# Moving the loads of two experts and of six bias rows behind another load in a mixture-of-experts kernel

## The reference

```python
def _L1_ffn_ref(x, Wr, We, be):          # x 16x256x512, Wr 512x8, We 8x512x512, be 8x512
    logits = jnp.einsum('bsd,de->bse', x, Wr)
    w, sel = jax.lax.top_k(logits, 2)
    w = jax.nn.softmax(w, axis=-1)
    gate = jnp.einsum('bsk,bske->bse', w, jax.nn.one_hot(sel, E, dtype=w.dtype))
    for e in range(E):
        out = out + gate[..., e:e + 1] * (jnp.einsum('bsd,df->bsf', x, We[e]) + be[e])
x = x + _L0_ffn_ref(_L0_cond_ref(x, ...), w1, w2, w3)
x = x + _L1_ffn_ref(_L1_cond_ref(x, cond), Wr, We, be)
```

## Time and profile before

| | us |
|---|---|
| median of three runs | 831.52 (828.22 to 833.4) |
| the profiled execution, device time | 832.25 |
| its span, first to last instruction | 830.5 |
| PE busy | 737.6 (89%) |
| DVE busy | 564.7 (68%) |
| POOL busy | 476.9 (57%) |
| ACT busy | 397.6 (48%) |

### The profile page before, as it was taken

The page is one execution under the profiler, slowest core; times in us unless marked ns, Lnnn a source line. Parts: engine busy times, 40 slices in busy tenths (PEclk is TensorE's granted clock), DMA queues, the critical chain, the costliest instruction groups (busy, mean ns, idle before and its releaser), DMA issues.

```text
span 830.5 us, 12599 instructions
## 1 busy us (share of the span) xinstructions
PE 737.6 (89%) x3954; PEld 431.8 (52%) x3954; DVE 564.7 (68%) x834; ACT 397.6 (48%) x635; POOL 476.9 (57%) x738
## 2 busy tenths in 40 slices
PE   1754599999999999999989999928899999999995
PEld 0112244444444444444436664326688888888884
DVE  2469999999998999998645441279753564545452
ACT  2056466667777777777612343215422434343432
POOL 1037889888888888886210000001457788888773
PEclk9987899999999999999999999958899999999998
DMA  9985147799999996554399899999459899999986
GB/s 359 387 318 164 26 89 141 142 182 178 180 173 167 183 192 129 131 115 90 83 215 225 94 114 239 130 79 322 114 102 166 146 167 165 167 165 168 164 162 89
DMA packets 230270, 137.50 MB, mean 166 GB/s; under 512 B 162798, under 2 KB 195054, under 8 KB 229054
## 3 DMA queue, kind: packets, MB, share of 16 engines
q1 hardware_dynamic: 210094, 99.94, 59.8%
q0 software_dynamic: 15456, 36.47, 24.2%
q10 hardware_dynamic: 4656, 0.30, 0.6%
HBM read 80.27 MB, written 35.42 MB: 139 GB/s over the span
## 4 chain that ended last, share of the span: by engine, by line
PE 58%; DVE 9%; DMA 7%; SPq 7%; POOL 7%; issue 7%; ACT 3%; POOLq 0%; DVEq 0%; ACTq 0%
PE PS L1597 21%; PE PS L1499 8%; PE PS L1448 6%; PE PS L1471 6%; PE PS L1460 6%; PE PS L1526 4%; PE PS L1577 3%; SPq L391 3%; DMA TZ<-in_taps 2%; DVE Ih L1094 2%; ACT Qh L827 1%; PE PS L1548 1%; DMA QyT<-Qy 1%; DMA QT<-Qh 1%; SPq L468 1%
## 5 line engine op out<-in xcount | busy, mean ns | idle before, releaser
L1597 PE MATMUL PS<-W,ZH 128*128 x552 | 178.4, 404 | 2.7 <-DVE ACC L1344 1.9
L751 POOL DMA_INDIRECT ZR<-z_scratch,IDG x69 | 69.2, 1003 | 154.9 <-DVE IDS L1315 134.2
L1448 PE MATMUL PS<-W,QyT 128*128 128x512 bf16 x512 | 123.8, 386 | 28.6 <-DMA QyT<-Qy 16.5
L760 POOL DMA_INDIRECT out_x<-YS,IDS x69 | 110.5, 1601 | 46.0 <-ACT YS L948 27.5
L1460 PE MATMUL PS<-W,QyT 128*128 128x512 bf16 x512 | 120.9, 379 | 0.0
L1471 PE MATMUL PS<-W,QT 128*128 128x512 bf16 x512 | 117.4, 383 | 3.5 <-DMA QT<-Qh 2.6
L948 ACT ACTIVATE YS<-YS,SG 128x512 f32<-128x512 f32 x69 | 50.1, 726 | 146.7 <-DVE YS L1376 146.7
L1597 PEld LDWEIGHTS PS<-W,ZH 128*128 128x128 f32 x552 | 99.5, 190 | 21.6 <-issue 3.9
L1597 PE MATMUL PS<-W,ZL 128*128 x276 | 109.0, 395 | 0.0
L1358 DVE TENSOR_TENSOR ZL<-PS,ZH 128x512 fp32r<-128x512 f32 x69 | 47.7, 691 | 78.4 <-ACT ZH L937 78.4
L1448 PEld LDWEIGHTS PS<-W,QyT 128*128 128x128 bf16 x512 | 49.4, 99 | 93.7 <-DMA QyT<-Qy 20.7
(11 more groups left out here) (230 smaller groups left out, 1062.7 us busy)
## 6 DMA issues: line engine op xcount, KB each, us to landing
XW<-out_x SPq DMA_DIRECT2D x64, 240.0 KB, 4.7
X<-in_x SPq DMA_DIRECT2D x32, 256.0 KB, 10.1
out_x<-X SPq DMA_DIRECT2D x32, 256.0 KB, 3.5
z_scratch<-ZZ SPq DMA_DIRECT2D x8, 1024.0 KB, 25.6
WRAW<-in_We SPq DMA_DIRECT2D x8, 1024.0 KB, 12.8
XR<-in_x SPq DMA_DIRECT2D x20, 256.0 KB, 4.3
stage<-in_w1T SPq DMA_DIRECT2D x4, 1024.0 KB, 7.9
stage<-in_w2T SPq DMA_DIRECT2D x4, 1024.0 KB, 12.3
```

The lines of the kernel that those rows point to most:

```text
L751: pool.indirect_dma_start(ZR[m % UZ][:], None, z_d, bass.IndirectOffsetOnAxis(IDG[:, m:m + 1].bitcast(U32), 0)) \
L760: pool.indirect_dma_start(x1_d, bass.IndirectOffsetOnAxis(IDS[:, m:m + 1].bitcast(U32), 0), YS[m % UN][:], None, compute_op=ALU.add).then_ ...
L1448: i = nc.tensor.matmul(GP[:, a, :], QyT[t][:, k, :], W12[:, k, o:o + CH], start=(k == 0), stop=(k == KD - 1))
L1597: x = nc.tensor.matmul(bank[i], zz[i % 2][:, k, :], W2[:, bass.ds(q, 1), part, k, :].rearrange("p o d -> p (o d)"), start=(k == 0 and n == ...
```

## The change

SP's stream is put into another order. Before the table is known, SP now issues experts 4 and 5 and only bias rows 0 and 1. After the `ACC` load it waits until the first piece of the bias (rows 0 and 1) has landed, and issues expert 6, bias rows 2 to 7, and expert 7. DVE gets one wait more: in slot 2, ahead of `YS`, for the second piece of the bias. No transfer is added in bytes; the bias load is two transfers where it was one.

```diff
-            for e in range(E // 2, E):
-                load_expert(e)
+            def load_be(first, last):
+                n = (last - first) * D
+                sp.dma_start(BEB[:, first:last, :].rearrange("p e d -> p (e d)"), bass.AP(be.tensor, first * D, [[0, P], [1, n]])) \
+                    .then_inc(be_in, 16)
+
+            load_expert(E // 2)
+            load_expert(E // 2 + 1)
             sp.wait_ge(z_out[0], 16 * NQ)
-            sp.dma_start(BEB[:].rearrange("p e d -> p (e d)"), bass.AP(be.tensor, 0, [[0, P], [1, E * D]])).then_inc(be_in, 16)
+            load_be(0, 2)
 
             sp.wait_ge(slots_done, 1)
             sp.dma_start(ACC[:], bass.AP(out.tensor, ND * D, [[OB * D, P], [1, D]])).then_inc(acc_in, 16)
+            sp.wait_ge(be_in, 16)
+            load_expert(E // 2 + 2)
+            load_be(2, E)
+            load_expert(E // 2 + 3)
             sp.wait_ge(first_done, 2)
             sp.wait_ge(acc_in, 16)
@@ (in DVE's slot)
                 dve.wait_ge(exp_done, m + 1)
+                if m == 2:
+                    dve.wait_ge(be_in, 32)
                 if m >= UN:
                     dve.wait_ge(y_out[i], 16 * (m // UN))
```

## The result

The changed kernel takes 835.36 us (median of ten runs, 833.99 to 838.79) against 830.24 us for the kernel before (ten runs, 828.22 to 833.4): a ratio of 1.0068 with a 95% interval of 1.0053 to 1.0083, or 5.1 us slower. The forecast was 831.1 us, in a range of 828.0 to 834.8. The time lies outside of it and on the other side of the kernel before.

A forecast was written before the change was run, and what follows sets the result against it. PE's chain was taken to bound the kernel, its waits at 578 to 600 us deciding. Gather 0 gave -0.38 us and all else 0; from the 831.52 median, less 0.4, the forecast was 831.1 us, range 828.0 to 834.8.

The forecast's parts named there:

- What bounds the kernel: PE's chain: only waits at 578 to 600 us count; the change can directly take only the 0.81 us gather wait.
- The ACC load: Load behind the table: lands earlier than 582.6, but its DVE reader starts only after `BEF`; worth 0.
- Gather 0: PE's first gather: lands after 3.9 us instead of 4.58, bounds 3.5 and 6.0; transposes start 0.76 us earlier.
- The rule on how transfers share: DMA engines alternate between queues packet by packet; new loads get about half the rate while gathers run.
- Clock: TensorE's clock in slot 0: falls near 582.4, rises near 589.25; 0.38 us of the gain survives, at most 0.76.
- the two cases that I priced: Clock rise in slot 0: as long after the transposes as before, 0.76 us survives; fixed at 589.25, 0.38.
- the clock does not fall: Rival, slot 0 and transposes on PE: full clock gains 3.2 us, 828.3 us in all; chance 0.06.
- Expert 6, the bias, SP: Loads behind `ACC`: expert 6 at 585.7, bias at 589.4 to 593.2, SP issues at most 6.8 us; each worth 0.
- Expert 7: Last load, read by ACT: lands at 593.9, just inside the 594.28 limit; worth 0, with nearly no room.
- the rival of equal shares: Expert 7 shares evenly with gathers, lands at 595.3, ACT waits: net +0.65 us, 832.2; late-expert case chance 0.25.
- The rival that I priced as the way to lose: Expert 7 late with ACT waiting for it: slower, under 1%, up to +5.3 us (836.8); chance 0.25.
- the signs of being wrong: ACT's wait for expert 7 past 594.7, another load keeping gather 0 or 1 longer, or another clock course at 582 to 590.

The follow-up runs named there:

- e4: Changed kernel, but SP waits until gathers 0 and 1 have landed before issuing expert 6, bias rows 2 to 7 and expert 7; ratio to before 1.0064.
- e7: Changed kernel, but SP issues expert 6, bias rows 2 to 7 and expert 7 only once `BEFF` is computed; ratio to before 0.9959.
- e13: Changed kernel with expert 6 ahead of the table; expert 7, then bias rows in short pieces, after `BEFF`; 830.92 us against 833.23 before, ratio 0.9975.
- e15: Repeat of e13 on a chip where the kernel before takes 842.75 us; 836.69 us, ratio 0.993.
- e14: The kernel before, unchanged, run for its trace on a chip where it takes 833.23 us; ratio 1.
- e18: Repeat of e8 on a chip where the kernel before takes 842.75 us; ratio 0.9954.
- e17: The kernel before, unchanged, run for its trace on a chip where it takes 842.75 us; ratio 1.
- e8: Changed kernel with experts 6 and 7 ahead as before, only bias rows 2 to 7 in 2 KB pieces behind `ACC`; ratio 0.9942 to before at 850.27 us.
- e12: Repeat of e8 beside the kernel before at 850.39 us; ratio 0.991.
- e9: The changed kernel itself on another chip; 844.61 us against 850.39 before, ratio 0.9935.

## Why the prediction was wrong, step by step

**What bounds the kernel: right.** Only what stands between PE and its work from 578 to 600 us counted, and 4.45 us at slot 3 reached the end: the device time moved by 5.1. The 0.7 us more are not traced: in the two profiled executions `IDG` started 2.5 us earlier in the changed kernel.

**The ACC load: right.** It landed 2.6 us after its issue instead of 4.8, and that was worth nothing.

**Gather 0: this step failed.** I took 3.9 us, with 3.5 and 6.0 as the bounds; it was 9.29. Three things went into it. First, the order of issue. The step says that the first bytes of expert 6 come at the gather's end, because I read expert 4's 7.5 us to landing as a late start of its bytes. Expert 6 landed 5.7 us after its issue; SP's packets moved from 1.2 us after `IDG` on (`ACC` first, expert 6 from about 2), and no gather packet before 3.1 us after `IDG` even in e4, where SP's queue was empty by then. Second, SP's issues. I gave them up to 6.8 us, from rows of a queue that was already full; they took 1.36, so that all 3.67 MB were queued before the gather's first packet. Third, the upper bound. The 6.0 was the slowest of 69 gathers, none of which had started behind megabytes of SP's queue. A maximum over rows that never meet the new condition bounds nothing; the loads' own bytes ahead of a gather's 3.5 us would have: 3.67 MB at my 420 GB/s are 8.7 us, 12.2 together. (The 420 GB/s themselves were read wrongly: 60 of the bias's 128 packets had moved before expert 7 landed at 577.0. From 577 to 580 us the changed kernel's queue, alone on engines that were 99% busy, moved 364 GB/s.)

**The rule on how transfers share: half right.** The Trainium skill describes turns packet by packet ("DMA: Bandwidth & Descriptors", section "Queues, rings and completion order"). From 581 us on the trace agrees as far as counts can, 63 packets against 73 and 153 against 147; it doesn't show in which order an engine took them. I used it for the loads' side and counted turns as halves of the bytes. With 12 KB against 4 KB packets they are far from that, and I didn't apply it to the gather, the only transfer that PE waited for. Before 581 us the trace shows no turns at all. Where no load behind `ACC` was issued yet and the bias had landed or was nearly through (before, e4, e7, e13, e15), a gather's first packet comes 3.1 us after `IDG`; in e14 it comes at 3.6, in e18 at 4.8, and in all others whose gathers were issued at 1.2 us at 5.5 to 6.7, with 1.0 to 3.7 MB behind `ACC` and with none (5.6 in e17, whose bias was issued 9.8 us ahead of `IDG`). Why it waits so long when loads are in flight stays open; three kernels meant to tell it (e8, e12, e18) met other loads in flight.

**Clock.** The granted clock was at its lower level from 5.7 to 15.9 us after `IDG`, around 580.7 and 590.9, where it had been from 4.9 to 11.7 before: 10.2 us instead of 6.9. That was no further loss, since the longer part fell in PE's wait, and slot 0 took 4.25 us. Of a gather that is not held I said that half of a 0.76 us gain survives slot 0. In e13 the transposes start 0.88 us earlier than before counted from `IDG` (5.01 against 5.89) and slot 3 0.41 earlier (21.61 against 22.02; I had 0.38), with a rise at 12.1, close to the 11.7 of before; part of that is luck, since PE also waited 0.64 us for gather 1 there. e4 shows neither of the two cases that I priced: the clock was low only from 4.2 to 7.7 us after `IDG`, slot 0 took 2.9 us instead of 4.52, and its matmuls ended 2.1 us earlier than before. So with an unheld gather more than the 0.76 us could be had, which I had only under "the clock does not fall" with a chance of 0.06.

**Expert 6, the bias, SP: right. Expert 7: later than forecast, but moot.** Expert 6 landed 5.7 us after its issue (I had 7.5) and the bias before DVE asked for it. Expert 7 landed 17.7 us after `IDG`; in the clock of the trace before that is 595.2, just where the rival of equal shares had it (595.3), and past the 593.9 of the forecast and the 594.28 that I held to be the limit. ACT didn't wait for it, since the late gather had shifted ACT too: it came to `high(7)` at 19.5. No wait for the bias in slot 2, and no wait of the scatters for SP. The rival that I priced as the way to lose was real, but only where the gathers were let through first (e4).

**The rivals** lacked the one that happened. I gave 0.25 to a loss of 0 to 5.3 us by ACT's wait and none to a gather held by the loads (it stood only among the signs of being wrong), though the profile of before showed the effect at its edge: the tail of the bias, less than 5 us of it, had made gather 0 1.1 us longer than in e4. My step used this only as a thing to be gained.

## What to carry to other kernels

When loads are moved out of the way of a short, urgent transfer, ask first what they will be ahead of in their new place: loads of 1.6 to 3.7 MB issued within half a microsecond of a gather from another queue put off its first packet by about 3 us, and then took about every other packet of the engines. Bound a transfer that meets a new neighbour by the neighbour's bytes and its own time, not by the slowest of its kind in a trace without that neighbour. And where an order depends on when a long store ends, compare it on more than one chip: here the same change was 0.7% slower on one and 0.65% faster on another.

## What the runs showed of the hardware that I had not expected

- A gather's packets didn't move for 4.4 to 5.1 us after its issue while loads of another queue that were issued up to half a microsecond ahead (changed kernel) or behind (e9) moved theirs (540 packets against none from 577 to 580 us); with the queue empty it was 1.9 us (e4). In e7 a gather issued 0.5 us ahead of such a load still took about 8.3 us. Then near equal counts of packets, whether SP's held 12 KB (63 against 73) or 2 KB (153 against 147).
- SP issued loads of 1 to 1.5 MB in 0.43 to 0.50 us each in the changed kernel, the second and third behind the others. Before, the first experts took 0.4 to 0.5 each too, the slowest of the four 2.1, and the bias behind all four 3.20.
- Chips differ in how long scattered stores take. The eight stores of `z` (1 MB each) took a median of 25.6 us in the trace before, 28.9 in e17 and 29.9 in e9 (24.4 to 25.7 in all traces from chips with the kernel before at 830 to 833, 28.8 to 30.3 in all others). Expert 4, which waits for the last of them, was issued at 560.3, 569.6 and 577.8 us: 17.2, 12.7 and 7.9 ahead of `IDG`.
- The clock's rise didn't come at a fixed time after the transposes: 5.8 us before, 5.3 in the changed kernel, about 7 in e13, 2.3 in e4. The lower level lasted 6.9 us before, 10.2 in the changed kernel, 6.8 in e13 and 3.5 in e4.
